# Attention scores of 16 heads: stacked bf16 parts against four-byte products of 32 rows on four heights of the array

## The chip, the cores and the metric

The kernel runs on one core of one Trainium2 chip, as one launch. The metric is the device time of a run in microseconds; less is better. Engines in the profile: PE (TensorE) with its weight loads PEld, DVE (VectorE), ACT (ScalarE), POOL (GpSimd) and SP (SyncE), which issues transfers.

## What is computed

64 sequences of 128 tokens, width 256, 16 heads of 16. In short:

```python
q = layernorm(x) @ Wq + bq; k = ctx @ Wk + bk; v = ctx @ Wv + bv
scores = einsum('bqhd,bkhd->bhqk', q, k) / sqrt(10)
scores = where(mask == 0, -1e9, scores)
x = x + tanh(g_xattn) * (softmax(scores) @ v)
x = x + tanh(g_ffn) * ffn(layernorm(x))   # 8 experts; each takes the 1024 tokens that score highest
```

## The kernel before, in words

The tokens go through in 64 batches of 128 (`b`), four to a group `g` of 512. A first part (attention) builds x after attention, the normalised rows and the router's scores; then a search finds each expert's tokens (some 573 to 640 us), and the experts run to the end. The change lies in the first part, but for one block of TensorE's work ahead of the experts.

`steps` runs every engine's own list once for each batch: a hand-written order, the same on each engine, software-pipelined. In step `b` TensorE makes the scores of batch b (`scores`, L938, into the two banks a_ps: 128 queries by 128 keys, four heads to a bank), and VectorE takes each row's maximum (`maximum`, L720, four a batch). TensorE transposes the maxima of batch b-1 (`max_t`, L1022), ScalarE and VectorE negate them in two bf16 parts (`neg_hi` L583, `neg_mid` L792), and SP writes them as rows of the stack of Q (`max_rows`, L360). With these rows TensorE makes the products of batch b-2 again, transposed (`scores_t_`, L951, banks b_ps), and ScalarE takes the exponential (`exp`, L576). Batch b-3 is multiplied with V (`values`, L967, 32 passes on four blocks of 32 columns), copied (`pv_copy`, L589), transposed back (`out_back`, L1030), and VectorE ends batch b-4 (`finish`, L802 to L821). The products of one kind stand in blocks of four heads, and the other work of the step stands between them.

`front` (L906, L917, L924) makes the next group's normalised x transposed (u = 0, 1), K (2, 3), Q (4, 5) and V (6, 7), two pieces a step, through the single bank f_ps and its pair of semaphores. A product of two four-byte operands is two passes (instructions) in the profile, each with its own weight load.

Scores must be exact to four bytes, so Q and K are cut in three bf16 parts (HI, MID, LO): VectorE makes K (`make_k` L701) and the rest of Q (`rest_q` L693), ScalarE rounds (`hi_q` L542, `mid_q` L547, `hi_k` L555, `mid_k` L560), GpSimd subtracts (`split_q` L475, `rest_k` L480, `split_k` L485). SP then copies the parts into stacks of 96 rows a head: six products of parts, of 16 rows each, plus a mask row and rows for the maxima (`stack_q` L334, `stack_k` L341 and L347):

```python
Q_ROWS = [HI, HI, HI, MID, MID, LO]
K_ROWS = [HI, MID, LO, HI, MID, HI]
...
pe.matmul(a_ps[q % 2][:, i * P:(i + 1) * P], q_st[g.p][0:A_K, h, tok], k_st[g.p][0:A_K, h, tok],
          start=True, stop=True)
```

GpSimd also computes the scale of each layer norm, a chain of 16 small operations (`ln1`, `ln2_scales`, L443 to L455), from VectorE's `stats` (L683, L687); ScalarE applies it (`normalise` L568, `normalise2` L596). SP's list holds the loads of a group (step j = 0), the store of x2 (1), the stacks (2) and the rows' store (3), with `max_rows` in each step.

Ahead of the experts TensorE runs `busy_parts` (L1693, L1697, L1701) before `left(1)` (L1593 to L1595): products into banks that nothing reads, of 128 rows, of 64 rows at two heights and of 32 rows at four heights. VectorE's `choose` (L1433) waits for `left`.

Of the kernel before, what the change touches and what calls it, by code (L numbers as in the profile page):

```python
# [34 lines left out]
P = 128  # L35
# [119 lines left out]
def attention(nc, ctx, w, x, ctx_t, mask, g_x, wq, bq, wk, bk, wv, bv, wg_t, out, rows, scores_t,  # L155
# [22 lines left out]
    ones_bf = sb("ones_bf", [HEADS, GT], BF16)  # L178
    gx_raw, gx = sb("gx_raw", [P, 1]), sb("gx", [P, 1])
    mask_nat = sb("mask_nat", [NB, P], I32)  # L180
    bias_nat = sb("bias_nat", [NB, P], BF16)
# [14 lines left out]
    neg_m = [sb(f"neg_m{i}", [HEADS, 2, P], BF16) for i in range(2)]  # L196
# [38 lines left out]
    q_hi, q_mid, q_lo = sem("q_hi"), sem("q_mid"), sem("q_lo")  # L235
    k_hi, k_r, k_mid, k_lo = sem("k_hi"), sem("k_r"), sem("k_mid"), sem("k_lo")
# [3 lines left out]
    mt_done, nhi_done, nmid_done = sem("mt_done"), sem("nhi_done"), sem("nmid_done")  # L240
# [51 lines left out]
    with nc.Block() as block:  # L292

        @block.sync
        def _(sp):
# [24 lines left out]
            def stacked(st, r):  # L320
                return st[r:SPLIT:len(Q_ROWS), :, :].rearrange("d (h k) t -> d h (k t)", k=KD)

            def flat(parts, part):
                return parts[:, part, :, :].rearrange("p k t -> p (k t)")

            def stack_q(g):
                if not g.ok:
                    return
                wait(sp, b_done, g.times(16, -16))
                for part, ready in ((HI, q_hi), (MID, q_mid), (LO, q_lo)):  # L330
                    sp.wait_ge(ready, g.times(2, 2))
                    for r, have in enumerate(Q_ROWS):
                        if have == part:
                            sp.dma_start(stacked(q_st[g.p], r), flat(q_part, part)).then_inc(s_q[g.p], 16)  # L334

            def stack_k(g):
                if not g.ok:
# [3 lines left out]
                sp.dma_start(k_st[g.p][MASK_ROW:MASK_ROW + 1, :, :],  # L341
                             mask_bias[0:1, bass.ds(g.tok, GT)].unsqueeze(1).to_broadcast([1, HEADS, GT])).then_inc(s_k[g.p], 16)
                for part, ready in ((HI, k_hi), (MID, k_mid), (LO, k_lo)):
                    sp.wait_ge(ready, g.times(2, 2))
                    for r, have in enumerate(K_ROWS):
                        if have == part:
                            sp.dma_start(stacked(k_st[g.p], r), flat(k_part, part)).then_inc(s_k[g.p], 16)  # L347
# [1508 lines left out]
```

## Time and profile before

| | |
|---|---|
| median of 3 runs | 941.08 us (940.59 to 945.37) |
| the profiled execution | 948.87 us, span 947.1 us |
| TensorE busy | 787.2 us (83%) |
| VectorE, ScalarE, GpSimd busy | 604.0, 540.5, 398.1 us |
| TensorE's mean granted clock | 0.929 |
| moved by DMA | 130.38 MB, mean 138 GB/s |

A row of the profile names line, engine, operation and tiles (out<-in), how many ran (x), busy time and the mean of one, then the idle time of the engine before them and what ended it. The granted clock is a share of 2.4 GHz; 0.50 is 1.2 GHz. Ends of matmuls are modelled.

### The profile page before, as it was taken

To read this page: it belongs to the slowest core of one execution; us is meant where nothing else is said; L and a number is where in the kernel's file an instruction comes from. 1 tells how busy PE (TensorE), PEld (TensorE's weight loads), DVE (VectorE), ACT (ScalarE), POOL (GpSimd) and SP (SyncE) were. 2 spreads that over 40 slices of the span, in tenths; PEclk is the share of its full clock that TensorE was granted. 3 is DMA by queue.
4 is the path that set the end of the run, shared out by engine and by line. 5 is a ranking of instruction groups with operands and counts; after the bars stand their busy time and mean duration, and the time that the engine had idled before them with its cause. 6 is when DMAs were issued, how large, how long until landed. Compare 5 with 4: busy or idle time off the path is not lost. (4 is left out here: it accounts for less than half of the span.)

```text
span 947.1 us, 22653 instructions
## 1 busy us (share of the span) xinstructions
PE 787.2 (83%) x7300; PEld 612.6 (65%) x7300; DVE 604.0 (64%) x1481; ACT 540.5 (57%) x1065; POOL 398.1 (42%) x791
## 2 busy tenths in 40 slices
PE   4388879889889988998898874149999999999994
PEld 2256657666666666666666752027888888888984
DVE  1266667767777777787777764966574574654540
ACT  2245465666666576666767573726556555555641
POOL 3342344334343434443353212233548448457415
PEclk9799899999999999999999895558999999999998
DMA  4954774795597579667864713413535536434214
GB/s 123 243 125 134 195 184 120 198 234 140 155 254 165 166 191 248 145 180 208 194 174 128 176 48 105 142 40 113 112 107 93 111 83 115 112 63 69 46 24 44
DMA packets 98899, 130.38 MB, mean 138 GB/s; under 512 B 13648, under 2 KB 61936, under 8 KB 98800
## 3 DMA queue, kind: packets, MB, share of 16 engines
q1 hardware_dynamic: 86544, 112.48, 44.5%
q0 software_dynamic: 12288, 17.05, 11.0%
q8 instruction: 37, 0.61, 0.3%
q14 instruction: 30, 0.25, 0.1%
HBM read 52.10 MB, written 25.71 MB: 82 GB/s over the span
## 5 line engine op out<-in xcount | busy, mean ns | idle before, releaser
L576 ACT ACTIVATE p_t<-b_ps 128x512 f32<-128x512 f32 x256 | 146.1, 587 | 105.7 <-PE b_ps L951 105.2
L720 DVE TENSOR_REDUCE m_sb<-a_ps 128x4 f32<-128x512 f32 x256 | 165.8, 676 | 31.5 <-PE a_ps L938 30.6
L1269 POOL DMA_INDIRECT out<-y,idx_add x64 | 100.3, 1568 | 110.7 <-ACT y L1328 100.0
L938 PE MATMUL a_ps<-k_st,q_st 97*128 97x128 bf16 x1024 | 103.8, 226 | 39.2 <-DMA q_st<-q_part 37.2
L951 PE MATMUL b_ps<-q_st,k_st 99*128 99x128 bf16 x1024 | 102.9, 225 | 13.6 <-ACT p_t L576 8.3
L938 PEld LDWEIGHTS a_ps<-k_st,q_st 97*128 97x128 bf16 x1024 | 73.1, 102 | 63.3 <-issue 38.0
L1638 PE MATMUL bank<-x_hi,w_hi 128*128 128x512 f32 x254 | 100.1, 394 | 0.0
L1638 PE MATMUL bank<-x_lo,w_hi 128*128 128x512 f32 x254 | 99.0, 390 | 0.0
L1638 PE MATMUL bank<-x_hi,w_lo 128*128 128x512 f32 x254 | 98.9, 389 | 0.0
L1506 DVE TENSOR_TENSOR act_h<-act_h,bank 128x512 f32<-128x512 f32 x64 | 44.0, 688 | 83.9 <-PE bank L1638 73.7
L1260 POOL DMA_INDIRECT xg<-rows_scratch,idx x64 | 67.8, 1059 | 61.8 <-issue 48.6
L951 PEld LDWEIGHTS b_ps<-q_st,k_st 99*128 99x128 bf16 x1024 | 72.4, 100 | 19.9 <-ACT p_t L576 9.0
L1316 ACT ACTIVATE act_h<-bank 128x512 f32<-128x512 f32 x64 | 38.3, 599 | 73.4 <-PE bank L1638 65.1
L1679 PE MATMUL bank<-w_hi,hid_hi 128*128 128x256 f32 x256 | 74.8, 292 | 0.0
L480 POOL TENSOR_TENSOR k_rest<-k_val,k_part 128x512 f32<-128x512 f32 x32 | 37.1, 1159 | 88.3 <-ACT k_part L555 88.3
L967 PEld LDWEIGHTS pv_ps<-p_t,v_aug 128*32 128x32 f32 x2048 | 53.5, 112 | 29.8 <-issue 28.9
L1679 PE MATMUL bank<-w_hi,hid_lo 128*128 128x256 f32 x256 | 71.4, 279 | 0.0
L1679 PE MATMUL bank<-w_lo,hid_hi 128*128 128x256 f32 x256 | 71.3, 278 | 0.0
L967 PE MATMUL pv_ps<-p_t,v_aug 128*32 128x128 f32 x2048 | 71.3, 281 | 0.0
L917 PE MATMUL f_ps<-xn_t,wq_sb 128*128 128x512 f32 x124 | 61.0, 614 | 8.2 <-DVE q_rest L693 6.8
L568 ACT ACTIVATE xn<-x_in,nm,y 128x256 f32<-128x256 f32 x64 | 34.6, 593 | 57.5 <-POOL nm L455 57.5
L924 PE MATMUL f_ps<-wv_sb,c_t 128*128 128x256 f32 x248 | 61.8, 392 | 5.1 <-DVE q_rest L693 3.1
(221 smaller groups left out, 1751.3 us busy)
## 6 DMA issues: line engine op xcount, KB each, us to landing
k_st<-k_part SPq DMA_DIRECT2D x96, 256.0 KB, 4.4
q_st<-q_part SPq DMA_DIRECT2D x96, 256.0 KB, 5.5
w<-in_w_t SPq DMA_DIRECT2D x24, 512.0 KB
rows_scratch<-xg SPq DMA_DIRECT2D x16, 528.0 KB, 5.6
x_in<-in_x SPq DMA_DIRECT2D x16, 512.0 KB, 5.5
c_t<-in_ctx_t SPq DMA_DIRECT2D x16, 512.0 KB, 5.4
x_res<-in_x SPq DMA_DIRECT2D x16, 512.0 KB, 4.5
out<-x SPq DMA_DIRECT2D x16, 512.0 KB, 3.9
```

Source lines behind the costliest of these rows:

```text
L576: act.activation(p_t[b.s % 2][:, 4 * q:4 * q + 4, :], b_ps[q % 2][:].rearrange("p (h s) -> p h s", s=P), ACT.Exp, scale=SCALE).then_inc(ex ...
L720: dve.tensor_reduce(m_sb[b.s % 2][:, 4 * q:4 * q + 4], a_ps[q % 2][:].rearrange("p (h s) -> p h s", s=P), AX_X, ALU.max).then_inc(max_done, 1)
L917: mm = pe.matmul(ps[:], wt[:, k, i * P:(i + 1) * P], src[:, k, :], start=(k == 0), stop=(k == KD - 1))
L924: mm = pe.matmul(ps[:, t * D:(t + 1) * D], c_t[g.p][:, k, tok:tok + P], wv_sb[:, k, :], start=(k == 0), stop=(k == KD - 1))
L938: mm = pe.matmul(a_ps[q % 2][:, i * P:(i + 1) * P], q_st[g.p][0:A_K, h, tok], k_st[g.p][0:A_K, h, tok], start=True, stop=True)
L951: mm = pe.matmul(b_ps[q % 2][:, i * P:(i + 1) * P], k_st[g.p][0:B_K, h, tok], q_st[g.p][0:B_K, h, tok], start=True, stop=True)
L967: mm = pe.matmul(pv_ps[VW * i:VW * (i + 1), q * P:(q + 1) * P], v_aug[b.group.p][:, b.j, h, :], p_t[b.s % 2][:, h, :], start=True, stop=True)
L1260: pool.indirect_dma_start(xg[e % 2][:, st, :], None, rows[:, :], bass.IndirectOffsetOnAxis(ap=idx[e % 2][:, st:st + 1], axis=0)).then_inc( ...
L1269: pool.indirect_dma_start(out[:, :], bass.IndirectOffsetOnAxis(ap=idx_add[e % 2][:, st:st + 1], axis=0), y[st][:], None, compute_op=ALU.ad ...
L1506: dve.tensor_tensor(act_h[n % 4][:], act_h[n % 4][:], h3_ps[n % 2][:, 0:SPAN], ALU.mult).then_inc(gate_done, 1)
L1638: mm = pe.matmul(ps[:, 0:SPAN], w_[e % 2][i][:, k, f], x_[e % 2][:, k, h * SPAN:(h + 1) * SPAN], start=(n == 0), stop=(n == len(passes_) - 1))
L1679: mm = pe.matmul(y_ps[st % 2][:, 0:D], h_[h][:, f, t], w_[e % 2][2][:, f, :], start=(n == 0), stop=(n == len(passes_) - 1))
```

## The change

Q and K stay four-byte values. Each head takes 32 rows: its 16 values on the even ones, the mask (ones in Q's tile) on row 1, the negated maximum (ones in K's) on row 31, zeros in K elsewhere. Four heads lie above one another in a tile of 128 rows, four tiles hold all 16. The scores are products of 31 or 32 rows at one of four heights. `scores(b, x)` now makes half of batch b's scores on two heights and half of batch b-2's transposed products on the other two, in turn, into four banks. ScalarE copies Q (`q_out`), VectorE makes K; nothing is split. SP copies four pieces for Q and four for K a group, and one row piece for the maxima; their bf16 second part goes. The order of the steps of all engines is new, the columns of Wq and Wk are laid out for it, and `busy_parts` gives way to six products of 512 columns. The helpers `rest_k`, `split_k`, `split_q`, `hi_k`, `mid_k`, `mid_q`, `rest_q` and `neg_mid` go. The diff's core (`neg_hi` becomes `negate`, with one row):

```diff
-HI, MID, LO = range(3)
-Q_ROWS = [HI, HI, HI, MID, MID, LO]
-K_ROWS = [HI, MID, LO, HI, MID, HI]
-SPLIT = len(Q_ROWS) * DH
-MASK_ROW, MAX_ROW = SPLIT, SPLIT + 1
-A_K, B_K = SPLIT + 1, SPLIT + 3
+RG = 32
+TILES = HEADS * RG // P
+MASK_ROW, MAX_ROW = 1, RG - 1
+A_K, B_K = RG - 1, RG
 MAGIC = 1597463007.0
-Q_SENT, K_SENT = 16 * 6, 16 * 7
+Q_SENT, K_SENT = 16 * 4, 16 * 5
...
-    q_rest, k_val, k_rest = sb("q_rest", [P, KD, GT]), sb("k_val", [P, KD, GT]), sb("k_rest", [P, KD, GT])
-    q_part, k_part = sb("q_part", [P, 3, KD, GT], BF16), sb("k_part", [P, 3, KD, GT], BF16)
-    q_st = [sb(f"q_st{p}", [P, HEADS, GT], BF16) for p in range(2)]
-    k_st = [sb(f"k_st{p}", [P, HEADS, GT], BF16) for p in range(2)]
+    q_val, k_val = sb("q_val", [P, KD, GT]), sb("k_val", [P, KD, GT])
+    q_st = [sb(f"q_st{p}", [P, TILES, GT]) for p in range(2)]
+    k_st = [sb(f"k_st{p}", [P, TILES, GT]) for p in range(2)]
...
+            def spread(st, val, m, s):
+                return st[0:P:2, 2 * m + s, :], val[s:P:2, m, :]
...
             def stack_q(g):
                 if not g.ok:
                     return
                 wait(sp, b_done, g.times(16, -16))
-                for part, ready in ((HI, q_hi), (MID, q_mid), (LO, q_lo)):
-                    sp.wait_ge(ready, g.times(2, 2))
-                    for r, have in enumerate(Q_ROWS):
-                        if have == part:
-                            sp.dma_start(stacked(q_st[g.p], r), flat(q_part, part)).then_inc(s_q[g.p], 16)
+                sp.sem_inc(passed, 1)
+                for m in range(KD):
+                    sp.wait_ge(q_done, g.times(2, m + 1))
+                    for s in range(2):
+                        to, from_ = spread(q_st[g.p], q_val, m, s)
+                        sp.dma_start(to, from_).then_inc(s_q[g.p], 16)
...
-                sp.dma_start(k_st[g.p][MASK_ROW:MASK_ROW + 1, :, :],
-                             mask_bias[0:1, bass.ds(g.tok, GT)].unsqueeze(1).to_broadcast([1, HEADS, GT])).then_inc(s_k[g.p], 16)
...
+                for m in range(KD):
+                    sp.wait_ge(k_done, g.times(2, m + 1))
+                    for s in range(2):
+                        to, from_ = spread(k_st[g.p], k_val, m, s)
+                        sp.dma_start(to, from_).then_inc(s_k[g.p], 16)
+                sp.dma_start(k_st[g.p][MASK_ROW:P:RG, :, :],
+                             mask_bias[0:1, bass.ds(g.tok, GT)].unsqueeze(1).to_broadcast([P // RG, TILES, GT])).then_inc(s_k[g.p], 16)
...
-                    sp.wait_ge(nmid_done, b.times(1, 1))
-                    for i in range(2):
-                        r = MAX_ROW + i
-                        sp.dma_start(q_st[b.group.p][r:r + 1, :, b.j * P:(b.j + 1) * P], neg_m[b.s % 2][:, i, :]).then_inc(s_m[b.s % 2], 16)
+                    sp.wait_ge(neg_done, b.times(1, 1))
+                    sp.dma_start(q_st[b.group.p][MAX_ROW:P:RG, :, b.j * P:(b.j + 1) * P], neg_m[b.s % 2][:]).then_inc(s_m[b.s % 2], 16)
...
-            sp.wait_ge(s_ones, 1)
-            for p in range(2):
-                load_const(q_st[p][MASK_ROW:MASK_ROW + 1, :, :], ones_bf[:], s_rows1)
-                for i in range(2):
-                    load_const(k_st[p][MAX_ROW + i:MAX_ROW + i + 1, :, :], ones_bf[:], s_rows1)
             sp.wait_ge(s_bias, 1)
             sp.dma_start(mask_bias.rearrange("a (b s) -> (a b) s", s=P), bias_nat[:]).then_inc(s_bias_st, 16)
             sp.wait_ge(s_bias_st, 16)
+            sp.wait_ge(s_ones, 4)
+            for p in range(2):
+                load_const(k_st[p][MAX_ROW:P:RG, :, :], q_st[p][MAX_ROW:P:RG, :, :], s_rows1)
...
-                if b.j == 2:
-                    stack_k(g.on(1))
                 if b.j == 3:
                     place_scores(g.on(-3))
                     store_rows(g.on(-3))
                 max_rows(b.back(1))
+                if b.j == 1:
+                    stack_k(g.on(1))
                 if b.j == 2:
...
+            for p in range(2):
+                pool.memset(k_st[p][:], 0.0).then_inc(s_ones, 1)
...
-            def hi_q(g, m):
+            def q_out(g, m):
                 if g.ok:
                     f_wait(g, 4 + m)
                     if m == 0:
                         last = g.on(-1)
                         wait(act, s_q[last.p], last.turn(Q_SENT, Q_SENT))
-                    act.activation(q_part[:, HI, m, :], f_bank(g, m)[:], ACT.Identity, bias=bq_sb[:, m:m + 1]).then_inc(q_hi, 1)
-            def mid_q(g, m):
-                if g.ok:
+                    act.activation(q_val[:, m, :], f_bank(g, m)[:], ACT.Identity, bias=bq_sb[:, m:m + 1]).then_inc(f_free[m], 1)
                     act.wait_ge(f_free[m], g.times(4, 3))
-                    act.activation(q_part[:, MID, m, :], q_rest[:, m, :], ACT.Copy).then_inc(q_mid, 1)
...
+                    act.sem_inc(q_done, 1)
...
+                    r = (q + 2) % 4
+                    act.activation(p_t[b.s % 2][:, 4 * r:4 * r + 4, :], b_ps[q % 2][:].rearrange("p (h s) -> p h s", s=P),
                                    ACT.Exp, scale=SCALE).then_inc(exp_done, 1)
...
             def step(act, b):
                 g, f = b.group, b.group.on(1)
-                exp(b.back(3), 3)
+                exp(b.back(2), 0)
+                negate(b.back(1))
+                exp(b.back(2), 1)
                 if b.j == 0:
                     if first(g):
                         xn_t_out(f, 0)
                     xn_t_out(f, 1)
+                if b.j == 2:
+                    q_out(f, 1)
+                pv_copy(b.back(3))
+                if b.j == 2:
+                    router_out(g.on(-3))
+                    normalise2(g.on(-2), (0, 1))
+                if b.j == 3:
+                    normalise2(g.on(-2), (2, 3))
+                exp(b.back(2), 2)
+                exp(b.back(2), 3)
                 if b.j == 1:
-                    mid_k(f, 0)
+                    q_out(f, 0)
                 if b.j == 2:
-                    hi_q(f, 1)
+                    normalise(g.on(2), (0, 1))
                 if b.j == 3:
-                    normalise(g.on(2), (2, 3))
-                neg_hi(b.back(1))
+                    xn_t_out(g.on(2), 0)
                 if b.j < 2:
                     xt2_copy(g.on(-3), b.j)
                 if b.j == 2:
...
+                    normalise(g.on(2), (2, 3))
...
+            for p in range(2):
+                dve.memset(q_st[p][:], 1.0).then_inc(s_ones, 1)
...
                     dve.wait_ge(s_c[g.p], g.turn(32, 32))
-                    wait(dve, k_r, g.times(2, m - 1))
+                    if m == 0:
+                        last = g.on(-1)
+                        wait(dve, s_k[last.p], last.turn(K_SENT, K_SENT))
                     dve.scalar_tensor_tensor(out=k_val[:, m, :], in0=f_bank(g, m)[:], scalar=bk_sb[:, m:m + 1],
                                              in1=mask_b[g.p][:], op0=ALU.add, op1=ALU.mult).then_inc(f_free[m], 1)
+                    dve.wait_ge(f_free[m], g.times(4, 2))
+                    dve.sem_inc(k_done, 1)
...
             def step(dve, b):
                 f = b.group.on(1)
                 maximum(b, 0)
+                maximum(b, 1)
                 if b.j == 1:
-                    stats(b.group.on(2), range(GB))
                     make_k(f, 1)
-                if b.j == 2:
-                    rest_q(f, 1)
                 if b.j == 3:
                     make_v(f, 1)
-                neg_mid(b.back(1))
-                maximum(b, 1)
-                maximum(b, 2)
                 finish(b.back(4))
                 if at_last(b, NG, 0):
                     again()
+                maximum(b, 2)
+                maximum(b, 3)
                 if b.j == 0:
                     make_k(f, 0)
                 if b.j == 1:
-                    rest_q(f, 0)
+                    stats(b.group.on(2), range(GB))
                 if b.j == 2:
                     make_v(f, 0)
-                maximum(b, 3)
...
+            def scores(b, x):
+                back = b.back(2)
+                if b.ok:
+                    g = b.group
+                    if x == 0 and b.j == 0:
+                        pe.wait_ge(s_q[g.p], g.turn(Q_SENT, Q_SENT))
+                        pe.wait_ge(s_k[g.p], g.turn(K_SENT, K_SENT))
+                    wait(pe, max_done, b.times(4, 2 * x))
+                if back.ok:
+                    if x == 0:
+                        pe.wait_ge(s_m[back.s % 2], back.turn(2, 16, 16))
+                    wait(pe, exp_done, back.times(4, 2 * x))
+                for t in range(TILES):
+                    for i in range(2):
+                        if b.ok:
+                            r, tok = RG * (2 * x + i), slice(b.j * P, (b.j + 1) * P)
+                            p = b.group.p
+                            mm = pe.matmul(a_ps[i][:, t * P:(t + 1) * P], q_st[p][r:r + A_K, t, tok], k_st[p][r:r + A_K, t, tok],
+                                           start=True, stop=True)
+                            if t == TILES - 1:
+                                mm.then_inc(a_done, 1)
+                    for i in range(2):
+                        if back.ok:
+                            r, tok = RG * (2 * (1 - x) + i), slice(back.j * P, (back.j + 1) * P)
+                            p = back.group.p
+                            mm = pe.matmul(b_ps[i][:, t * P:(t + 1) * P], k_st[p][r:r + B_K, t, tok], q_st[p][r:r + B_K, t, tok],
+                                           start=True, stop=True)
+                            if t == TILES - 1:
+                                mm.then_inc(b_done, 1)
...
-                    if b.j in (1, 2) and back.ok:
-                        pe.wait_ge(xt2_out, back.times(2, b.j))
+                    if b.j > 1 and back.ok:
+                        pe.wait_ge(xt2_out, back.times(2, b.j - 1))
                     pe.wait_ge(f_free[1], b.group.times(4, 4))
                     pe.wait_ge(f_free[0], b.group.times(4, 4))
                     wait(pe, pv_out, b.times(1))
-                pe.wait_ge(exp_done, b.times(4, q + 1))
+                    pe.wait_ge(exp_done, b.times(4, 4))
...
             def step(pe, b):
                 g = b.group
+                scores(b, 0)
+                max_t(b)
+                if b.j == 0 and first(g):
+                    front(g.on(1), 0)
+                front(g.on(1), 2 * b.j + 1)
                 for q in range(4):
-                    scores(b, q)
-                    if q == OT_AT:
-                        out_back(b)
-                    scores_t_(*((b.back(2), q - 1) if q else (b.back(3), 3)))
-                    if q in (0, 2):
-                        u = 2 * b.j + q // 2 + 1
-                        if u == 1 and first(g):
-                            front(g.on(1), 0)
-                        front(*((g.on(1), u) if u < 8 else (g.on(2), 0)))
-                    if q == 2:
-                        for i in range(4):
-                            values(b.back(3), i, g.on(-3))
-                        if b.j == 1:
-                            router(g.on(-3), b)
-                        if b.j == 2:
-                            scores_back(g.on(-3), b)
-                    if q == 0:
-                        max_t(b)
-                    if q == 0 and b.j < 2:
-                        xn2_back(g.on(-3), b.j, b)
+                    values(b.back(3), q, g.on(-3))
+                if b.j == 2:
+                    router(g.on(-3), b)
+                scores(b, 1)
+                front(*((g.on(1), 2 * b.j + 2) if b.j < 3 else (g.on(2), 0)))
+                out_back(b)
+                if b.j < 2:
+                    xn2_back(g.on(-3), b.j, b)
+                if b.j == 2:
+                    scores_back(g.on(-3), b)
...
-        busy_parts()
+        busy(t_ps[1], 6)
...
```

## Rows read from the trace of the kernel before

**Rows 1.** Table by stretches: PE, PEld, DVE, ACT, POOL busy (x), clock, DMA, GB/s

```profile
140.00:500.00 360.00, 321.04 (x3751) 233.83 (x3751) 271.67 (x645) 235.56 (x491) 148.58 (x417) 0.97 0.72 186
600.00:640.00 40.00, 11.61 (x82) 7.60 (x82) 31.24 (x120) 18.14 (x46) 7.87 (x8) 0.50 0.20 63
```

**Rows 2.** TensorE's waits, 140:500: total us, times, longest

```profile
PE a_ps L938 <- DMA q_st<-q_part: 13.9, 8, 2.8
PE b_ps L951 <- ACT p_t L576: 8.3, 14, 0.7
PE f_ps L906 <- ACT xn L568: 5.8, 10, 0.6
PE f_ps L917 <- DVE q_rest L693: 4.4, 11, 0.5
```

**Rows 3.** Groups of TensorE, 140:500 us

```profile
L938 PE MATMUL a_ps<-k_st,q_st 97*128 97x128 bf16 x704 | 70.7, 224 | 15.9 <-DMA q_st<-q_part 13.9 <-DVE m_sb L720 2.0
```

**Rows 4.** Timeline of TensorE, 350:362: start, us, what

```profile
350.61 1.94 PE L917 MATMUL f_ps<-xn_t,wq_sb 128*128 128x512 f32 x4
...
354.16 0.39 PE L951 MATMUL b_ps<-q_st,k_st 99*128 99x128 bf16 x4
...
358.06 0.61 PE L1030 MATMUL o_ps<-ident,o_t 128*128 128x128 f32 x4
...
359.00 1.99 PE L924 MATMUL f_ps<-wv_sb,c_t 128*128 128x256 f32 x8
360.93 0.86 PE L967 MATMUL pv_ps<-p_t,v_aug 128*32 128x128 f32 x24
```

**Rows 5.** Timeline of TensorE, then of VectorE, 632:640

```profile
632.51 1.67 PE L1701 MATMUL bank<-ones 32*128 32x128 f32 x24
...
634.18 0.17 PE L1595 MATMUL bank<-place,less_before 128*128 128x1 f16 x1
...
638.40 0.31 PE L1603 MATMUL bank<-count,from_last 128*128 128x128 f16 x1
...
637.16 0.35 DVE L1433 SCALAR_TENSOR_TENSOR chosen<-place,bank,tied 128x128 f16<-128x128 f16 x1 [3.92 <-remote]
...
639.33 0.49 DVE L1443 TENSOR_SCALAR begun<-slot,bank 128x1024 f16<-128x1024 f16 x1 [1.09 <-PE bank L1603]
```

**Rows 6.** Groups over the span: ScalarE, GpSimd, VectorE

```profile
L560 ACT ACTIVATE k_part<-k_rest 128x512 bf16<-128x512 f32 x32 | 20.3, 634 | 15.8 <-POOL k_rest L480 15.8
...
L480 POOL TENSOR_TENSOR k_rest<-k_val,k_part 128x512 f32<-128x512 f32 x32 | 37.1, 1159 | 88.3 <-ACT k_part L555 88.3
...
L693 DVE SCALAR_TENSOR_TENSOR q_rest<-f_ps,bq_sb,q_part 128x512 f32<-128x512 f32 x31 | 23.3, 751 | 29.8 <-ACT q_part L542 29.8
```

**Rows 7.** Transfers by issue: count, KB each, median us to landing

```profile
q_st<-q_part SPq DMA_DIRECT2D x96, 256.0 KB, 5.5
...
q_st<-neg_m SPq DMA_DIRECT2D x128, 4.0 KB, 4.3
```

**Rows 8.** Timeline of VectorE: two maxima, ends of finish

```profile
355.32 1.28 DVE L720 TENSOR_REDUCE m_sb<-a_ps 128x4 f32<-128x512 f32 x2
...
360.26 0.23 DVE L802 RECIPROCAL rden<-o_ps 128x16 f32<-128x16 f32 x1
...
362.12 0.18 DVE L821 BATCH_NORM_AGGREGATE mv<-stats 128x2 f32<-128x6 f32 x1 [0.19 <-DVE stats L817]
```

**Rows 9.** Timeline of GpSimd: first and last of 16

```profile
357.67 0.23 POOL L443 TENSOR_SCALAR v<-mv 128x4 f32<-128x4 f32 x1
...
363.62 0.23 POOL L455 TENSOR_SCALAR nm<-t 128x4 f32<-128x4 f32 x1 [0.20 <-POOL t L454]
```

**Rows 10.** Timeline of GpSimd, SP and TensorE, 0:46

```profile
0.82 3.54 POOL L435 MEMSET v_aug<- 128x2048 f32 x2 [0.29 <-POOLq L1846]
...
31.94 4.94 SPq L334 DMA_DIRECT2D q_st<-q_part  x6
...
43.55 0.58 PE L938 MATMUL a_ps<-k_st,q_st 97*128 97x128 bf16 x4 [12.11 <-DMA q_st<-q_part]
```

More of the change, by code:

```diff
@@ L429, in _ @@
                 sp.wait_ge(s_out[p], 16 * (NG // 2))
[L430 removed]
+            sp.wait_ge(s_rows1, 16 * 2)
         @block.gpsimd
@@ L500, in _ @@
             ln1(Group(0, 0, NG))
-            g = Group(0, 0, NG)
-            for m in range(KD):
-                rest_k(g, m)
-                split_k(g, m)
-            for m in range(KD):
-                split_q(g, m)
             ln1(Group(0, 1, NG))
@@ L510, in step @@
                 g = b.group
-                for m in range(KD):
-                    if b.j == 1:
-                        rest_k(g.on(1), m)
-                        split_k(g.on(1), m)
-                    if b.j == 2:
-                        split_q(g.on(1), m)
                 if b.j == 1:
@@ L617, in _ @@
                 xn_t_out(g, k)
-            for m in range(KD):
-                hi_k(g, m)
-                mid_k(g, m)
             act.wait_ge(s_wq, 32)
             for m in range(KD):
-                hi_q(g, m)
-                mid_q(g, m)
+                q_out(g, m)
             normalise(Group(0, 1, NG), range(GB))
@@ L687, in stats @@
                     dve.bn_aggr(mv1[:, t, :], stats1[:, t, :]).then_inc(s_mv1, 1)
-            def rest_q(g, m):
-                if g.ok:
-                    dve.wait_ge(q_hi, g.times(2, m + 1))
-                    wait(dve, q_lo, g.times(2, m - 1))
-                    dve.scalar_tensor_tensor(out=q_rest[:, m, :], in0=f_bank(g, m)[:], scalar=bq_sb[:, m:m + 1],
-                                             in1=q_part[:, HI, m, :], op0=ALU.add, op1=ALU.subtract).then_inc(f_free[m], 1)
             def make_k(g, m):
@@ L832, in _ @@
                 make_k(g, m)
-            dve.wait_ge(s_wq, 32)
-            for m in range(KD):
-                rest_q(g, m)
             dve.wait_ge(s_wv, 32)
@@ L926, in front @@
                 mm.then_inc(f_done, 1)
-            def scores(b, q):
-                if not b.ok:
-                    return
-                g = b.group
-                if q == 0 and b.j == 0:
-                    pe.wait_ge(s_q[g.p], g.turn(Q_SENT, Q_SENT))
-                    pe.wait_ge(s_k[g.p], g.turn(K_SENT, K_SENT))
-                wait(pe, max_done, b.times(4, q - 1))
-                for i in range(4):
-                    h, tok = 4 * q + i, slice(b.j * P, (b.j + 1) * P)
-                    mm = pe.matmul(a_ps[q % 2][:, i * P:(i + 1) * P], q_st[g.p][0:A_K, h, tok], k_st[g.p][0:A_K, h, tok],
-                                   start=True, stop=True)
-                mm.then_inc(a_done, 1)
@@ L942, in scores_t_ @@
-            def scores_t_(b, q):
-                if not b.ok:
-                    return
-                g = b.group
-                if q == 0:
-                    pe.wait_ge(s_m[b.s % 2], b.turn(2, 32, 32))
-                wait(pe, exp_done, b.times(4, q - 1))
-                for i in range(4):
-                    h, tok = 4 * q + i, slice(b.j * P, (b.j + 1) * P)
-                    mm = pe.matmul(b_ps[q % 2][:, i * P:(i + 1) * P], k_st[g.p][0:B_K, h, tok], q_st[g.p][0:B_K, h, tok],
-                                   start=True, stop=True)
-                mm.then_inc(b_done, 1)
+            def scores(b, x):
[27 more added lines that the diff above has]
+                                mm.then_inc(b_done, 1)
@@ L974, in m_free @@
                 if use.ok:
-                    pe.wait_ge(nmid_done, use.times(1, 1))
+                    pe.wait_ge(neg_done, use.times(1, 1))
             def router(g, b):
@@ L1014, in max_t @@
                         pe.wait_ge(f_free[1], 4)
-                    if b.j == 2 and g.ok:
-                        pe.wait_ge(r_out, g.times(1, 1))
-                        pe.sem_inc(passed, 1)
                     if b.j == 3 and g.ok:
                         pe.wait_ge(st_out, g.times(1, 1))
-                    wait(pe, nmid_done, use.times(1))
+                    wait(pe, neg_done, use.times(1))
                     pe.wait_ge(max_done, use.times(4, 4))
@@ L1024, in out_back @@
             def out_back(b):
-                use = b.back(4)
+                use = b.back(3)
                 if use.ok:
@@ L1034, in xn2_back @@
                 if g.ok:
-                    last = b.back(4)
+                    last = b.back(3)
                     pe.wait_ge(pv_out, last.times(1, 1) if last.ok else NB)
-                    if k == 1 and not b.back(3).ok:
+                    if k == 1:
                         pe.wait_ge(xt2_out, g.times(2, 1))
@@ L1818, in columns @@
         lead = m.shape[:-1]
-        m = m.reshape(*lead, P // DH, KD, DH)
-        return np.moveaxis(m, (-3, -2, -1), (-1, -3, -2)).reshape(*lead, D)
+        m = m.reshape(*lead, P // RG, KD, RG // DH, DH)
+        return np.moveaxis(m, (-4, -3, -2, -1), (-3, -4, -1, -2)).reshape(*lead, D)
     return {
```

100 lines of the change are left out of this document (9 added, 91 removed).

## The prediction

> **What bounds the kernel now.** I read, in this order, the table by stretches, what TensorE waited for, the groups of one line, and a stretch of the timeline on each engine. From 140 to 500 us TensorE is busy 321 of 360 us at 0.97 of its clock, VectorE 272, ScalarE 236, GpSimd 149 [rows 1]: TensorE is nearest to its limit, no other engine reaches 80%. Its waits in that stretch name what is late: the parts of Q that transfers bring, an exponential, the normalised x, the rest of Q [rows 2]. Those four sum to 32.4 us. L938 ran 704 times there [rows 3], 16 a batch, so 44.0 batches: a step (one batch) takes 8.18 us.
>
> How much of a step is stream shows in groups of neighbours [rows 4], less the length of one (its mean in the page's groups): bf16 products (0.39 - 0.22) / 3 = 0.056 us each; the values' passes, four column blocks at once, (0.86 - 0.28) / 23 = 0.025; L1030 (0.61 - 0.28) / 3 = 0.11; L917 (1.94 - 0.61) / 3 = 0.44; L924 (1.99 - 0.39) / 7 = 0.23. L924's last pass starts at 360.60 and streams 0.22, L967 starts at 360.93: 0.1 for a change of the array's shape. Per step: scores 32 x 0.056 = 1.8; values 32 x 0.025 + 2 x 0.1 = 1.0; L1030 0.43; L1022 0.1; front (8 x 0.11 + 16 x 0.44 + 16 x 0.22) / 4 = 2.85; the group's L1041, L984, L993 about 0.4. Sum 6.6. The other 1.6 us are waits (32.4 / 44 = 0.74 by rows 2) and the ends of matmuls that a wait exposes.
>
> **The change, part by part.**
>
> *Products.* Each becomes two passes over 32 rows. The nearest row is in this very trace: L1701, 24 such passes on four heights and four banks, busy 1.67 us, 0.44 for one [rows 5]: (1.67 - 0.44) / 23 = 0.053 a pass at a granted clock of 0.50 [rows 1], so 0.027 at full clock. 64 passes a step are 1.73 us, what the bf16 products cost today; the stream gains nothing. It loses at the edges: two blocks a step, instead of products strewn between other work, make four changes of shape at 0.1, and two first weight loads that nothing covers. No row shows that load at 32 rows; L924's first pass in rows 4 adds 0.1 to its seven starts (0.23 for 0.22 each), so between 0 and 0.2, I take 0.1. After: 6.6 - 1.8 + 1.73 + 0.4 + 0.2 = 7.1 us.
>
> *Parts and stacks.* ScalarE loses L560 and its likes L555 and L547, six a group at 0.63: 0.95 us a step; GpSimd six like L480 at 1.16: 1.74; VectorE L693 and the small L792, 0.65 [rows 6]. None of them is the bound: worth nothing as busy time, hidden under TensorE. What counts is the chain. It was product, high part, rest, middle part, low part, transfer; now product, copy, transfer. SP issues four transfers of Q for six (0.6 to 0.8 us each, landing 5.5 us on [rows 7, 10]), and no later than step 2, so Q has a whole step to spare: the 13.9 us (0.32 a step) go, and the 4.4 us for the rest of Q (0.10). K's issue moves from step 2 to step 1 behind the maxima's rows, where it delays nothing that is due within the step. If this cover were gone, the 0.42 would be back.
>
> *Order.* A block needs both a banks and both b banks free. First half: L1022, a front piece and the values (0.1 + 1.76 + 1.0) give VectorE 2.9 us for two maxima (1.28) and ScalarE the same for two exponentials and the negation (about 1.4): covered. Second half: a front piece and L1030 give 2.2 us, and the two maxima queue behind finish, L802 to L821, 2.04 us [rows 8]. VectorE's loop is 1.28 + 0.75 (K or V) + 2.04 + 1.28, then TensorE's block of 1.3 and its end of 0.27: 6.9, under 7.1 by 0.2. So VectorE is late where front is a transpose (j = 3 and 0), which covers 1.3 less. At j = 3 ScalarE also stands behind GpSimd: the statistics move to the end of step 1, the chain of 16 small operations takes 6.2 us, 357.67 to 363.85 [rows 9], then four L568, and the exponentials behind them come about 0.9 us late. The maxima's row: negated 2.1 us into the step, landed 4.3 later [rows 7], 6.5 of 7.7, just hidden. I put what waits are left at 0.6 us a step; bounds 0 (every cover holds) and 1.1 (today's 1.6 less 0.42). So 7.7 us a step, between 7.1 and 8.2, for 8.18: -0.48 x 60 steps = -29 us.
>
> *Start.* The first product comes at 43.55, 6.7 us after the last of Q's six transfers was issued [rows 10]. Six transfers of ones become two, Q's chain loses its parts; GpSimd first clears 16 KB more per partition, as long as L435's 3.54 us, and holds its first chain up by 1.7. Net -5, bounds -8 and +1.
>
> *End of attention.* The last four steps have no front; VectorE's loop of 6.0 us takes the place of 5.5 now: +2.
>
> *The probe.* L1693 to L1701 stand before `left(1)`. VectorE idles 3.92 us before L1433, which waits for that [rows 5]. The six 512-column passes put in their place take 2.6 us at half clock: between -0.8 and -3.9, taken -3.
>
> **Sum.** -29 - 5 + 2 - 3 = -35. The profiled execution took 948.87 us, so 914; the median of the runs, 941.08, lies 7.8 lower: **906**.
>
> **A rule against it.** The probe's starts say that four heights work at once. The Trainium skill ("TensorE: Matmul & The Clock Gate", Part 3: Packing small matmuls) states 3.07 times, measured, for four row tiles of 32 rows. By that the 64 passes would cost 2.25 us for 1.73, and the sum would come near 938.
>
> **Rivals.**
> - *Heights overlap only in part* (0.11). If one height in four takes its turn, 1.73 becomes 2.31: +0.58 a step, 60 steps, +35: 941. For it: the probe ran on constants at half clock. Against: its 24 passes fill 1.67 us without a gap. The rule above is this one.
> - *Heights take turns: slower* (0.11). L1595, right behind the probe, is recorded until 634.35, but VectorE, which waits for it, starts at 637.16, 2.8 us later [rows 5]. If the 24 passes really took 1.3 + 2.8 us, one costs 0.17 at half clock, 0.086 at full: 64 are 5.5, +3.8 us a step, some 62 steps, +235: 1140. It decides from 0.035 us a pass on (0.5 us a step). Against: L1603, issued after TensorE had idled 3 us, is also answered 0.6 us late (638.71 to 639.33), so something else may delay that stretch.
> - *Coarse hand-overs* (0.11). Each half waits for VectorE, since maxima 2 and 3 stand behind finish: steps of 8.1 to 8.4 us, 930 to 948, centre 940.
> - *Nothing waits* (0.15). 7.1 us a step, another -36, with cover for the last steps: 870 to 880.
> - *Forecast* (0.52). 885 to 925.
>
> **How the numbers follow.** A measurement of this kernel tells about 0.5% (4.7 us) from no change. Faster: 0.52 + 0.15, and 0.08 of the two rivals near 941, 0.75. Within 0.5%: 0.09 of those two. Slower: their last 0.05 and the turns' 0.11, 0.16. The range 874 to 948 takes in the forecast, both middle rivals but for 0.03, and most of the best case; outside stay the turns (0.11) and some 0.05 below.
>
> **What would show it.** Right: no L475 to L485 work on GpSimd; passes starting every 0.027 us at full clock; steps of 7.7 us; no wait for Q's transfer, the largest being a block that waits for m_sb or p_t; the first product near 38 us; a DMA share well under 0.72. Wrong: passes over 0.035 us; maxima that start long after the last recorded pass of their block; a granted clock under 0.9 from 140 to 500 us, which at half clock would add a stream of 7 us to every step.

## The result, and the profile after

The changed kernel took 928.55 us (median of 4 runs, 927.44 to 930.08), the kernel before 943.18 beside it: ratio 0.9847, 95% interval 0.981 to 0.9884. It is 14.6 us faster where 35 were forecast; 906 was too low, though 928.55 lies in the range of 874 to 948. The profiled execution took 929.12 us (span 927.4) against 948.87 (947.1).

The stretch of [rows 1], from 140 to 500 us, in the changed kernel (same columns):

```profile
140.00:500.00 360.00, 322.76 (x5106) 235.02 (x5108) 238.29 (x570) 207.07 (x425) 72.86 (x352) 0.95 0.36 122
```

VectorE, ScalarE and GpSimd are relieved, and the DMA share halves, as forecast. TensorE is busy as before. What it waited for there, to set against [rows 2]:

```profile
PE b_ps L875 <- issue: 16.7, 4, 4.5
PE a_ps L867 <- issue: 12.7, 4, 3.3
PE a_ps L867 <- DVE m_sb L654: 6.8, 6, 1.4
PE a_ps L867 <- ACT p_t L526: 1.0, 1, 1.0
```

The waits for Q's transfer, for the rest of Q and for the normalised x are gone; that for the exponentials is 1.0 us, and that for the maxima has grown from 2.0 to 6.8. In place of the others stand eight waits that no engine and no transfer ended: "issue", 29.4 us, in two sorts of four. One pair in the timeline of TensorE:

```profile
348.43 0.38 PE L867 MATMUL a_ps<-k_st,q_st 31*128 31x128 f32 x2
348.44 0.38 PE L875 MATMUL b_ps<-q_st,k_st 32*128 32x128 f32 x2
348.64 0.28 PE L867 MATMUL a_ps<-k_st,q_st 31*128 31x128 f32 x2
348.65 0.28 PE L875 MATMUL b_ps<-q_st,k_st 32*128 32x128 f32 x2
348.75 0.28 PE L867 MATMUL a_ps<-k_st,q_st 31*128 31x128 f32 x2
...
350.02 0.60 PE L952 MATMUL o_ps<-ident,o_t 128*128 128x128 f32 x4
353.96 0.38 PE L867 MATMUL a_ps<-k_st,q_st 31*128 31x128 f32 x2 [3.33 <-issue]
...
359.17 0.58 PE L875 MATMUL b_ps<-q_st,k_st 32*128 32x128 f32 x1 [4.49 <-issue]
```

Two things are to be seen. Four passes start every 0.11 us (348.64, 348.75): 0.027 each at full clock, the value taken in the prediction. And TensorE stands still for 3.33 us, issues some 15 passes, and stands for another 4.49. The same stretch in the timeline of VectorE, maxima alone (two a row; 341.99, 350.18 and 364.34 hold the third and fourth of a batch):

```profile
341.99 1.29 DVE L654 TENSOR_REDUCE m_sb<-a_ps 128x4 f32<-128x512 f32 x2 [1.13 <-PE a_ps L867]
345.56 1.29 DVE L654 TENSOR_REDUCE m_sb<-a_ps 128x4 f32<-128x512 f32 x2 [0.30 <-PE a_ps L867]
350.18 1.29 DVE L654 TENSOR_REDUCE m_sb<-a_ps 128x4 f32<-128x512 f32 x2
360.52 1.29 DVE L654 TENSOR_REDUCE m_sb<-a_ps 128x4 f32<-128x512 f32 x2 [9.06 <-PE a_ps L867]
364.34 1.29 DVE L654 TENSOR_REDUCE m_sb<-a_ps 128x4 f32<-128x512 f32 x2 [0.30 <-PE a_ps L867]
```

From 341.99 to 350.18 are 8.19 us, from there to 364.34 14.16. Read this way (one batch's fourth maximum to the next's), the four intervals of a group take about 8.2, 7.5, 8.2 and 6.1 us, the fourth being that which leads over to the next group. But behind groups 5, 7, 9 and 11 the fourth takes 14.4, 14.3, 14.2 and 13.9. Those are the four places where `Fori` in `steps` branches back (groups 4 to 13, two a turn), and the first stop stands right behind the branch. At about 8.2 us over the usual each they make 33. The clock adds to it; table by stretches, around that turn:

```profile
350.60:359.10 8.50, 0.74 (x16) 0.53 (x15) 0.86 (x2) 1.00 (x3) 3.10 (x16) 0.81 0.66 220
359.10:363.00 3.90, 3.83 (x54) 3.17 (x54) 2.21 (x5) 1.81 (x4) 0.00 (x0) 0.54 0.03 6
363.00:370.00 7.00, 7.00 (x89) 4.27 (x81) 4.08 (x8) 3.50 (x7) 0.00 (x0) 1.00 0.22 77
```

TensorE did nearly nothing for 8.5 us, and for the next 3.9 it was granted 0.54, nearly all of it the lower level of 1.2 GHz. The last view is the list of DMA queues. The queue that carries instructions, in the kernel before and in the changed one (packets, MB, share):

```profile
q8 instruction: 37, 0.61, 0.3%
```

```profile
q8 instruction: 85, 1.39, 0.6%
```

A packet is 16.4 KB. In the stretch of [rows 1] the kernel before runs 3751 / 44.0 = 85 passes a step, the changed one 32 more, each with a weight load: 8 steps are some 1,360 against 1,880 instructions a turn. Counted in the trace with TensorE's waits and register operations (130 and 117 a turn), a turn is 1,494 instructions before and 1,993 in the changed kernel. When the packets come says more than how many: from 235 to 495 us, inside the loop, the kernel before brings none at all, and the changed one

```profile
q8 instruction: 37, 0.61, 1.0%
```

By this reading the difference of the two profiles, 19.7 us, is made up so: the first maximum 4.9 earlier (44.24 to 39.30), the way from there to the end of batch 0's maxima 1.9 shorter, the next 60 steps 9.5 (488.0 to 478.5, where 29 were forecast), the last three 0.7 longer (2 forecast), and from the last maximum to the end 4.0 less (390.3 to 386.3, 3 forecast).

### The profile page after: what moved, and what is told of

The parts are those of the page before. It is cut to its first block and busy times, and to the rows that moved or that the text cites. A ratio compares the mean times of both kernels' runs of the same rounds, so it can differ in the third digit from the quotient of the medians.

```text
span 927.4 us, 26147 instructions
## 1 busy us (share of the span) xinstructions
PE 795.2 (86%) x9314; PEld 614.8 (66%) x9314; DVE 563.4 (61%) x1386; ACT 496.8 (54%) x969; POOL 291.8 (31%) x697
## 5 line engine op out<-in xcount | busy, mean ns | idle before, releaser
L526 ACT ACTIVATE p_t<-b_ps 128x512 f32<-128x512 f32 x256 | 143.4, 587 | 100.0 <-PE b_ps L875 99.8
L867 PE MATMUL a_ps<-k_st,q_st 31*128 31x128 f32 x2048 | 154.6, 289 | 32.4 <-issue 12.7
L867 PEld LDWEIGHTS a_ps<-k_st,q_st 31*128 31x128 f32 x2048 | 129.0, 191 | 60.8 <-issue 50.5
L875 PE MATMUL b_ps<-q_st,k_st 32*128 32x128 f32 x2048 | 153.7, 287 | 17.9 <-issue 16.7
L875 PEld LDWEIGHTS b_ps<-q_st,k_st 32*128 32x128 f32 x2048 | 128.0, 190 | 19.8 <-issue 19.1
L435 POOL TENSOR_SCALAR v<-mv 128x4 f32<-128x4 f32 x32 | 7.3, 228 | 373.1 <-DVE mv L624 232.5
L539 ACT ACTIVATE o_t<-pv_ps 128x512 f32<-128x512 f32 x64 | 38.2, 597 | 55.3 <-PE pv_ps L892 55.2
L838 PE MATMUL f_ps<-c_t,wk_sb 128*128 128x512 f32 x124 | 63.6, 637 | 0.0
```

The source lines that it names most:

```text
L526: act.activation(p_t[b.s % 2][:, 4 * r:4 * r + 4, :], b_ps[q % 2][:].rearrange("p (h s) -> p h s", s=P), ACT.Exp, scale=SCALE).then_inc(ex ...
L838: mm = pe.matmul(ps[:], wt[:, k, i * P:(i + 1) * P], src[:, k, :], start=(k == 0), stop=(k == KD - 1))
L867: mm = pe.matmul(a_ps[i][:, t * P:(t + 1) * P], q_st[p][r:r + A_K, t, tok], k_st[p][r:r + A_K, t, tok], start=True, stop=True)
L875: mm = pe.matmul(b_ps[i][:, t * P:(t + 1) * P], k_st[p][r:r + B_K, t, tok], q_st[p][r:r + B_K, t, tok], start=True, stop=True)
```

## The experiments

**Theory:** TensorE's loop body (its instructions for one turn) has outgrown what is kept of its program, so each turn fetches it again and TensorE stands still meanwhile. **Rivals:** something that recurs every second group (a buffer, a transfer, another engine's turn) holds TensorE there; or the four heights and the new order bring the stall.

**1. The loop written out.**

```diff
-        with eng.Fori(2, NG // 2 - 1, 1) as k:
-            for s in range(2 * GB):
-                step(eng, Batch(k, s, NB))
-        for g in range(NG - 2, NG + 4):
+        for g in range(4, NG + 4):
...
-    VIA_TILE = NG - 5
+    VIA_TILE = 1
```

> The changed kernel with the 40 looped steps written out, so that no engine takes a branch back (the scores of all groups but the first are then written where they belong, without a tile between). Theory (TensorE waits for its instructions at each turn of the loop, 14.2 us for the last step of a turn where 6.1 is usual, four times, then half clock for 7 to 10 us): the four long steps go, 4 x 8.2 = 33, and some 3 for the clock: 892 to 897 us. Rival (something that recurs every second group, a buffer, a transfer or another engine, holds TensorE there): the four long steps stay, 924 to 932. Second rival (the time is lost at the turn, but is given back later in waits for VectorE): 900 to 915.

Measured: 891.59 us, ratio to the kernel before 0.9463 (0.9437 to 0.949). The waits and the stretch from 140 to 500:

```profile
PE a_ps L864 <- ACT p_t L523: 13.3, 14, 1.4
PE a_ps L864 <- DVE m_sb L651: 2.7, 3, 1.0
```

```profile
140.00:500.00 360.00, 344.01 (x5724) 252.41 (x5722) 261.84 (x629) 226.29 (x468) 73.93 (x365) 1.00 0.37 128
```

No "issue" is left, the clock is 1.00, and ten groups on end take 29.88 us each with intervals of 8.40, 7.56, 8.13 and 5.80. The loss, 37 us, was nearly all at the turns: the 60 steps take 442.6 us for 478.5, 35.9 less, of which the four intervals at the turns are 33.6 (14.2 for 5.8 each). Its instruction queue:

```profile
q8 instruction: 75, 1.23, 0.6%
```

This kernel reads every instruction once, with no loop, and needs 75 packets for its 18,628 passes and loads: 248 a packet. The looped one needed 85 for the same work. So it fetched again what it had run already.

**2. The same in the kernel before** (the same edit).

> The kernel before, with its 40 looped steps written out in the same way. Theory (only the longer loop body of the changed kernel stalls): its own turns show no long step, so nothing to gain: 936 to 943 us. Rival (any turn of any loop costs TensorE this): 905 to 915.

Measured: 948.56 us, ratio 1.006 (1.003 to 1.009): no gain, some 6 us lost, outside the 936 to 943 that were expected. It needs 59 packets (14,600 passes and loads, 247 a packet) where the loop needs 37, so the kernel before keeps its body from turn to turn. The loss stands in its waits for transfers, 24.7 us for q_part and 7.8 for the maxima's rows, against 13.9 and 3.1 before. Why they come later without the loop was not looked into.

**3. A shorter loop** (`Fori(4, NG // 2 - 1, 1)`, groups 4 to 7 written out, `by_tile` to match).

> The changed kernel with the loop cut to its last three passes (groups 8 to 13; groups 4 to 7 written out). Theory: the long steps at the ends of groups 5 and 7 go, those of groups 9 and 11 stay at 14 us each: 2 x 8.2 + 1.5 less, 909 to 913 us. Rival (a recurring dependency): all four stay, 924 to 932.

Measured: 902.18 us, ratio 0.9563 (0.9533 to 0.9593), 7 us better than expected. Groups 5 and 7 end with 5.8 and 6.3 us, groups 9 and 11 with 10.1 and 10.4. The place is as the theory has it, the size is not: its waits of TensorE show one stop a turn where the changed kernel has two.

```profile
PE a_ps L870 <- issue: 6.4, 2, 3.4
```

The body is the same. Where in a packet the branch lands may decide whether there is a second stop; that wasn't tried.

**4. Which engine's loop it is.** First TensorE alone written out; in the other run the condition is `is not`, and the four others are written out. `by_tile` goes by the group's number in both.

```diff
-        with eng.Fori(2, NG // 2 - 1, 1) as k:
...
+        if eng is nc.tensor:
+            for g in range(4, NG - 2):
+                for j in range(GB):
+                    step(eng, Batch(g // 2, 4 * (g % 2) + j, NB))
+        else:
+            with eng.Fori(2, NG // 2 - 1, 1) as k:
```

> The changed kernel with the 40 looped steps written out on TensorE alone; the four other engines keep their loop. Theory (it is TensorE's own program that is fetched again at a turn): no long steps, 892 to 897 us, near the 891.6 of all engines written out; the q8 queue at about 75 packets. Rival (another engine, SP's transfers above all, is late at its turn and TensorE shows it): the four long steps stay, 922 to 932.

> The reverse: TensorE keeps its loop, the four other engines have the 40 steps written out. Theory: the four steps of about 14 us stay, 922 to 932 us, and q8 stays at about 85 packets. Rival (another engine's turn): 892 to 897 us.

Measured: 893.47 us (ratio 0.9496, 0.9452 to 0.954) and 927.29 us (0.9857, 0.981 to 0.9904), with 75 and 85 packets. With the other engines written out, the intervals at the turns still take 14.2, 14.1, 14.3 and 13.8 us, and TensorE's waits read

```profile
PE b_ps L880 <- issue: 16.4, 4, 4.5
PE a_ps L872 <- issue: 11.8, 4, 3.4
```

It is TensorE's own loop, and nothing else's. The packets on q8 go with it too: they are fewer where TensorE alone is written out, and stay at 85 where the four others are.

**5. The stall put into the kernel before.** Its products L917 in pieces, which streams the same columns with more instructions:

```diff
-                    for k in range(KD):
-                        mm = pe.matmul(ps[:], wt[:, k, i * P:(i + 1) * P], src[:, k, :], start=(k == 0), stop=(k == KD - 1))
+                    for c in range(0, GT, PIECE):
+                        for k in range(KD):
+                            mm = pe.matmul(ps[:, c:c + PIECE], wt[:, k, i * P:(i + 1) * P], src[:, k, c:c + PIECE], start=(k == 0), stop=(k == KD - 1))
```

With PIECE = 64, 128 and 256:

> The kernel before with the front's products L917 in eight pieces of 64 columns in place of one of 512: same products, same columns, 112 more of them in the loop body, about as many TensorE instructions a turn as the changed kernel has. Theory (the number of instructions in the body decides): four steps at the ends of groups 5, 7, 9 and 11 get longer by 7 to 10 us than their like in other groups; the time is 33 more for that, plus 0 to 1.7 us a step for weight loads that the short pieces don't cover, 960 to 1080 us. Rival (the stall comes from the changed kernel's order or its four heights): the steps at the turns are no longer than the others.

> The kernel before with L917 in four pieces of 128 columns in place of one of 512: 48 more products in the loop body where the run with pieces of 64 had 112 more. Theory (the body is kept between two passes of the loop as long as it fits, and is fetched again when it doesn't; this one is 1,686 instructions where 1,494 fit and 1,942 did not): no long steps at the ends of groups 5, 7, 9 and 11, and 38 to 46 packets of the instruction queue q8. Rival (each instruction more costs at the turn): those steps 1 to 2 us longer than their like, and 60 packets or more.

> The kernel before with L917 in two pieces of 256 columns in place of one of 512: 16 more products in the loop body, 1,558 TensorE instructions as compiled, where 1,494 caused no stall and 1,686 did. It narrows the limit. If the limit is six packets of the instruction queue (six times 256 = 1,536): long steps of 12 us and more at the ends of groups 5, 7, 9 and 11, 70 packets or more, 975 to 990 us. If it lies above 1,558: no long steps, 38 or 39 packets, 938 to 950 us.

Each of the three ran once. The body is counted in the trace as above; an interval goes from the end of one batch's fourth maximum to the next's.

| body, instructions | kernel | packets | interval behind groups 5, 7, 9, 11 (turns) | behind 6, 8, 10, 12 | us |
|---|---|---|---|---|---|
| 1,494 | before | 37 | 8.5, 8.0, 6.8, 8.0 | 6.3, 6.8, 6.8, 6.7 | 941.81 |
| 1,558 | PIECE 256 | 38 | 7.3, 6.8, 6.6, 6.6 | 7.8, 7.7, 6.3, 7.7 | 941.79 |
| 1,686 | PIECE 128 | 76 | 17.3, 16.8, 16.4, 16.5 | 7.7, 7.5, 7.2, 7.2 | 990.35 |
| 1,942 | PIECE 64 | 80 | 12.7, 13.6, 14.0, 14.2 | 9.4, 9.4, 9.3, 9.0 | 1065.98 |
| 1,993 | changed | 85 | 14.4, 14.3, 14.2, 13.9 | 6.1, 6.1, 6.1, 6.1 | 928.55 |

The stall can be switched on in the kernel before, without heights, without a new order: the second rival falls. It is a step, not a slope: 1,558 instructions cost nothing, 1,686 cost 9 to 10 us a turn, and packets go from 38 to 76. From 235 to 495 us the run with 256 brings no packet, as the kernel before, and the run with 128 brings 32. My expectation missed the limit: pieces of 128 were to fit. It lies between 1,558 and 1,686, and so is not the six packets (1,536) of the last expectation. TensorE's waits in the run with 128:

```profile
PE a_ps L940 <- issue: 20.9, 4, 6.5
...
PE pv_ps L1043 <- issue: 8.5, 4, 3.3
```

With 64 the body is longer and the stall shorter (3 to 5 us, where 7 to 10 were expected), but a step there is some 1.6 us longer than in the kernel before (groups 6, 8, 10 and 12 take 38.2 to 38.6 us for 31.9 to 32.1), probably from weight loads that short pieces don't cover; that may leave more time to fetch ahead. Shown is only that body size alone doesn't set the length of the stall. Nor does the packet's own time: in the changed kernel's first stop above (350.60 to 353.96) one packet of q8 comes and takes 0.9 us of the 3.3, while the DMA engines are 0.66 busy with other transfers. Whether these hold the fetch up was not tried.

**6. The heights, two at a time.** On the kernel of experiment 1, in each half first the products of the maxima, then the transposed ones:

```diff
                     for i in range(2):
                         if b.ok:
...
+                for t in range(TILES):
                     for i in range(2):
                         if back.ok:
```

> The changed kernel written out, with the products for the maxima (two heights) issued ahead of those for the transposed heads (the other two) in each half, in place of mixing them: same products, order changed. Theory (a pass of 32 rows streams 0.11 us and four heights work at once, 0.027 us a pass; two heights give 0.054): 64 passes cost 1.73 more a step, 60 steps: 985 to 1000 us. Rival (the array takes a pass every 0.027 us whatever the heights): 890 to 895.

Measured, in one run: 950.18 us, 59 more than experiment 1, by order alone, but short of the 985 to 1000 expected; a group takes 33.72 us for 29.88, 0.96 a step where 1.73 was expected. In the timeline of TensorE one half reads

```profile
357.27 0.82 PE L864 MATMUL a_ps<-k_st,q_st 31*128 31x128 f32 x10
357.83 0.38 PE L873 MATMUL b_ps<-q_st,k_st 32*128 32x128 f32 x2
...
358.17 0.83 PE L873 MATMUL b_ps<-q_st,k_st 32*128 32x128 f32 x11
358.92 1.99 PE L842 MATMUL f_ps<-wv_sb,c_t 128*128 128x256 f32 x8
```

The half lasts 1.65 us (357.27 to 358.92) against 1.10 in experiment 1 (359.18 to 360.28). The first ten passes take (0.82 - 0.28) / 9 = 0.06 each, so two heights do give 0.054 to 0.06; but L873 starts 0.56 in, when ten of the 16 passes of the maxima have started. All 16 stand ahead of it in the program, so the passes on the other two heights overtake the last six, and in the middle of the half four heights are at work after all. That is what the expected 1.73 had wrong: the two halves cost 1.10 a step, and TensorE's waits shrink beside it, from 16.0 to 4.9 us between 140 and 500. So mixing is worth 59 us, and the rival (a pass every 0.027 whatever the heights) falls.

**7. The probe alone.** In the kernel before, `busy_parts()` replaced by `busy(t_ps[1], 6)`.

> The kernel before with its probe (24 products of 32 rows on four heights and the 16 ahead of them) replaced by the six 512-column passes that the changed kernel has there; nothing else. The prediction's term: 3 us less, between 0.8 and 3.9, all of it between the last maximum and the end of the span (390.9 us in the kernel before, 387.0 in the changed one). Theory (the 3.9 us between these two ends are the probe): 387 there, 937 to 939 us. Rival (the end is shorter for another reason): 390 to 391 there, 940 to 942.

Measured: 942.8 us, ratio 0.9986 (0.9963 to 1.0009), where 937 to 939 were expected: the run's time doesn't show it. In the profile, from the last maximum to the end takes 388.2 us for 390.3. In place it is clearer. VectorE's two L1433, which stand on either side of the probe, in this run:

```profile
623.12 0.35 DVE L1433 SCALAR_TENSOR_TENSOR chosen<-place,bank,tied 128x128 f16<-128x128 f16 x1 [0.34 <-PE bank L1595]
...
632.69 0.36 DVE L1433 SCALAR_TENSOR_TENSOR chosen<-place,bank,tied 128x128 f16<-128x128 f16 x1 [0.32 <-PE bank L1595]
```

They start 9.6 us apart. In the kernel before the first of them is

```profile
623.99 0.36 DVE L1433 SCALAR_TENSOR_TENSOR chosen<-place,bank,tied 128x128 f16<-128x128 f16 x1 [0.33 <-PE bank L1595]
```

and the second starts at 637.16 [rows 5], 13.2 us later. The probe cost 3.6 there, and the 2.8 us by which VectorE was late behind L1595 went with it. What made it late stays open: the heights themselves don't, for the maxima start 0.30 us after their products in the rows above.

**8. Better than both.** In experiment 1 TensorE still waits about once a group, 1.0 us, before the second half of j = 3. Both engines that it needs are only just ready. On ScalarE, and then on VectorE:

```diff
+                exp(b.back(2), 2)
+                exp(b.back(2), 3)
                 if b.j == 3:
                     normalise2(g.on(-2), (2, 3))
-                exp(b.back(2), 2)
-                exp(b.back(2), 3)
...
+                finish(b.back(4))
                 if b.j == 3:
                     make_v(f, 1)
-                finish(b.back(4))
```

> The changed kernel written out, with two moves in the last step of each group (j = 3): ScalarE normalises x2 behind its third and fourth exponentials, VectorE finishes a batch ahead of adding the bias of V. Theory (TensorE's 1.0 us of waiting, once a group, is for these two engines, whose last operations before it end within 0.3 us of each other): 0.5 to 0.7 us a group, 15 groups: 881 to 885 us. Rival (another operation takes their place as the late one, or front now waits for the bias of V): 889 to 893.

Measured: 884.37 us, ratio 0.9391 (0.9369 to 0.9414). A group takes 29.39 us for 29.88 (the interval that leads to j = 3 7.62 for 8.13), and the wait for the exponential is halved:

```profile
PE a_ps L864 <- ACT p_t L523: 6.7, 14, 0.9
PE a_ps L864 <- DVE m_sb L651: 2.7, 3, 1.0
```

## Why the prediction was right in part and wrong in size

**What failed is a step that isn't there.** The part on products costs 64 passes for 32 by what they stream, 1.73 us for 1.8, and by shape changes; it never asks what 32 more passes with their loads do to the length of TensorE's loop. They take the body from 1,494 to 1,993 instructions, past a limit between 1,558 and 1,686, and that cost 37 us, more than the whole forecast gain. The trace of before could have raised it: q8 brought 37 packets for 14,600 passes and loads, 395 a packet, more than the 248 that the written-out kernel gets through for each, and none at all from 235 to 495 us, so instructions were being kept between turns, and what is kept has an end. It could not price it. The Trainium skill ("Runtime: NRT & Kernel Launch", Instruction fetch mechanics) says that a taken branch whose target lies outside the current window of two pages makes the engine wait for a fetch. The runs agree on the wait, some 8 us a turn here, but not on so small a window: its blocks are 256 instructions, and bodies of 1,494 and 1,558 were kept. The same section of the Trainium skill gives TensorE room for 2,048 instructions, by which the 1,993 would still fit; the runs put the limit below 1,686, and the measurement decides.

**Without the turns the gain was larger than forecast, not smaller.** Experiment 1 against before is 50 us, in the profiles 57.4 (947.1 to 889.7). Step by step:

| term | forecast | measured |
|---|---|---|
| a pass of 32 rows, four heights | 0.027 us | 0.027 |
| the two blocks of scores in a step | 2.33 (1.73 + 0.4 + 0.2) | 2.20 (two of 1.10) |
| stream of a step | 7.1 | 7.47 less 0.33 of waits (16.0 us, 49 steps): 7.14 busy |
| waits left a step | 0.6 (0 to 1.1) | 0.33 |
| a step | 7.7 for 8.18 | 7.47 (29.88 / 4) |
| 60 steps | -29 | -45.4 written out, -9.5 with the loop |
| start | -5 | first maximum -4.9 |
| end of attention | +2 | +0.7 |
| probe | -3 | -3.6 in place, -2.1 in its own run's tail |

The stream came out to within 0.04 us, though 7.14 is busy time: a wait exposes the end of the pass ahead of it, about 0.17 us (0.28 less 0.11) or 0.06 a step, which the prediction counted with the waits, so 7.08 and 0.39 by its terms. *Waits* is the term that was mis-sized: 0.33 a step for 0.6, which makes the step 8.18 - 7.47 = 0.71 shorter and not 0.48, 43 us over 60 steps and not 29. I had counted VectorE late at j = 3 and at j = 0 and added for hand-overs; but one wait a group is left. It is the one that the prediction named, the exponentials "about 0.9 us late" at j = 3: 13.3 us in 14 waits, 0.95 each. *Start* came out right in part by luck: the first product starts at 34.36 for 43.55, 9 us earlier (near 38 was forecast), but VectorE's first maximum then waits for gx, which ScalarE makes at 39.09, behind four `normalise` that wait until 37.11 for GpSimd's chain:

```profile
39.30 1.29 DVE L654 TENSOR_REDUCE m_sb<-a_ps 128x4 f32<-128x512 f32 x2 [6.88 <-ACT gx L573]
```

That was the late one next, and I had named none for the first maximum; and the first batch gains 1.9 us more behind it, which no term held. *Parts and stacks* is right: no transfer is among the waits from 140 to 500. What is left is the exponentials (13.3 us for 8.3 before) and the maxima (2.7 for 2.0), 16.0 us where [rows 2] had over 32.

**The rivals.** Partial overlap, 941, and turns of heights, 1140, both fall by the rows at 348.64 to 348.75: the trace has 0.027 us a pass, a quarter of the 0.11 that a pass of 128 columns takes alone [rows 4]. By the 3.07 times of the Trainium skill ("TensorE: Matmul & The Clock Gate", Part 3: Packing small matmuls), which it states for 512 columns, a pass would be 0.035 us, an estimate; the measurement decides. Coarse hand-overs, 930 to 948, came nearest in time and is wrong in cause: away from the turns a step takes 7.5 to 7.65 us (groups of 29.9 to 30.6), not 8.1 to 8.4. The forecast had the mechanism of a step right and that of the loop not at all; the time measured, between its 925 and the 930 of this rival, belonged to no case. Of its signs of failure, a granted clock under 0.9 did not show either (0.95): four dips of a few us don't reach it.

## What to carry to other kernels

When a change trades few large matmuls for many small ones inside a hardware loop, count the instructions of the body on that engine as well as the columns they stream; here the stall took 37 of the 50 us that the change brings without it. A wait named "issue" that returns once a turn, and more packets on the instruction queue than the program written out needs, are how it looks in a profile. Small products on different heights paid here only when issued in turn: the order alone was 59 us (950.18 for 891.59, one run), and without it nothing would have been gained on the 941.81 of the kernel before.

## What the runs showed of the hardware that was not expected

- TensorE's loop body was kept between turns at 1,558 instructions and fetched again at 1,686 (38 and 76 packets of 16.4 KB). The stall is one or two stops a turn, of 2 to 6.5 us, on TensorE's own loop alone; in the stretch looked at, about half clock for some 4 us followed.
- Products of 32 rows at four heights ran four at once without loss: 0.027 us a pass of 128 columns at 2.4 GHz; a half with two heights issued ahead of the other two took 1.65 us for 1.10.
- Passes on different heights did not start in the order of the program: in that half, L873 starts at 357.83, ahead of the last six of the 16 passes of L864 that stand before it.
